# First projection of a two-layer transformer block: the bias of values and drift layer added by VectorE from a table on all partitions

## What is computed

```
Q = (x @ Wq + bq).reshape(B, S, Hn, Dh)
K = (x @ Wk + bk).reshape(B, S, Hn, Dh)
V = (x @ Wv + bv).reshape(B, S, Hn, Dh)
...
h = x @ dp_w1 + dp_b1
mu = h.mean(-1, keepdims=True)
var = ((h - mu) ** 2).mean(-1, keepdims=True)
h = (h - mu) / jnp.sqrt(var + LN_EPS) * ln_g + ln_b
```

## Time and profile before

| | |
|---|---|
| median of three runs | 3087.31 us (3075.47 to 3087.85) |
| the profiled execution, its time | 3087.55 us |
| its span in the trace | 3085.7 us |
| stage `project` in the trace | from about 31 to 205 us |
| mean granted clock of TensorE | 0.916 of full speed |

### The profile page before, as it was taken

The page is one execution under the profiler, slowest core; times in us unless marked ns, Lnnn a source line. Parts: engine busy times, 40 slices in busy tenths (PEclk is TensorE's granted clock), DMA queues, the critical chain, the costliest instruction groups (busy, mean ns, idle before and its releaser), DMA issues. The chain is left out here.

```text
span 3085.7 us, 91077 instructions
## 1 busy us (share of the span) xinstructions
PE 2676.6 (87%) x35080; PEld 1642.8 (53%) x35080; DVE 2270.2 (74%) x4339; ACT 1582.0 (51%) x2164; POOL 374.7 (12%) x341
## 2 busy tenths in 40 slices
PE   6869999899989998999999777999977778229997
PEld 3322566666656665567556424555535555117765
DVE  3539899799979987998989705565657897775776
ACT  2320677677767776777767671111115666204442
POOL 1245000000000000000000200000002222202333
PEclk9985899999999999999999897999988888659998
DMA  4244011101111011110110001000001222313341
GB/s 139 72 98 81 3 27 27 27 5 26 26 27 26 6 26 26 27 27 5 26 26 7 6 11 55 14 27 16 11 2 45 65 72 78 112 40 108 103 112 54
DMA packets 130633, 130.27 MB, mean 42 GB/s; under 512 B 76418, under 2 KB 107780, under 8 KB 125060
## 3 DMA queue, kind: packets, MB, share of 16 engines
q1 hardware_dynamic: 124548, 120.93, 16.6%
q10 hardware_dynamic: 4224, 4.19, 0.4%
q0 software_dynamic: 1536, 0.40, 0.1%
HBM read 78.41 MB, written 46.66 MB: 41 GB/s over the span
## 5 line engine op out<-in xcount | busy, mean ns | idle before, releaser
L677 DVE TENSOR_REDUCE attn_pm<-attn_MS 128x1 f32<-128x512 f32 (+3 forms) x2304 | 1334.0, 638 | 189.1 <-PE attn_MS L721 162.1
L661 ACT ACTIVATE attn_PT<-attn_ES 128x1024 f32<-128x1024 f32 (+5 forms) x1152 | 1039.1, 951 | 372.9 <-PE attn_ES L756 370.3
L721 PE MATMUL attn_MS<-attn_KX,attn_QX 96*32 96x512 bf16 (+11 forms) x9216 | 1038.3, 375 | 11.1 <-DVE attn_pm L677 5.6
L756 PE MATMUL attn_ES<-attn_QX,attn_KX 99*32 99x512 bf16 (+8 forms) x9216 | 773.0, 362 | 51.2 <-issue 20.1
L771 PE MATMUL attn_OP<-attn_PT,attn_VH 128*17 128x512 f32 (+3 forms) x4608 | 648.5, 565 | 0.2 <-ACT attn_PT L661 0.2
L721 PEld LDWEIGHTS attn_MS<-attn_KX,attn_QX 96*32 96x32 bf16 x9216 | 411.6, 97 | 300.7 <-issue 128.3
L756 PEld LDWEIGHTS attn_ES<-attn_QX,attn_KX 99*32 99x32 bf16 x9216 | 376.6, 97 | 194.7 <-ACT attn_PT L661 55.4
L1131 PE MATMUL l0out_ring<-l0out_w,l0out_sT 128*128 128x512 f32 x512 | 224.9, 592 | 0.0
L771 PEld LDWEIGHTS attn_OP<-attn_PT,attn_VH 128*17 128x17 f32 x4608 | 189.8, 98 | 48.9 <-issue 3.1
L716 PE MATMUL attn_MS<-attn_maskb,identb 128*32 128x128 bf16 (+3 forms) x2048 | 168.6, 206 | 37.8 <-DMA attn_QX<-qk_parts 25.4
L609 POOL TENSOR_SCALAR attn_parts<-attn_nmT 32x128 bf16<-32x128 f32 x16 | 22.6, 1411 | 1387.9 <-DVE attn_nmT L686 1387.9
(11 more groups left out here) (278 smaller groups left out, 2952.9 us busy)
## 6 DMA issues: line engine op xcount, KB each, us to landing
attn_KX<-qk_parts SPq DMA_DIRECT2D x96, 128.0 KB, 6.9
attn_QX<-qk_parts SPq DMA_DIRECT2D x96, 128.0 KB, 7.6
vk_beta<-front_vk SPq DMA_DIRECT2D x8, 1024.0 KB, 3.9
kq_transposed<-front_qkG SPq DMA_DIRECT2D x8, 1024.0 KB, 4.5
delta_VK<-vk_beta SPq DMA_DIRECT2D x32, 256.0 KB, 2.8
delta_QK<-kq_transposed SPq DMA_DIRECT2D x32, 256.0 KB, 2.9
attn_out<-attn_OS SPq DMA_DIRECT2D x128, 34.0 KB
x_res<-in_L_attn_x_dram ACTq DMA_DIRECT2D x8, 512.0 KB, 8.2
```

What stands on the lines that cost most here:

```text
L661: nc.scalar.activation(PT[u % NPT][:, 512 - wa:512 + wb], ES[half][:, 512 - wa:512 + wb], ACT.Exp, scale=DH ** -0.5).then_inc(exp_done, 1)
L677: nc.vector.tensor_reduce(pm[r][:, i, c:c + 1], MS[slot][:, 0:w], AX.X, ALU.max).then_inc(max_taken, 1)
L721: last = nc.tensor.matmul(MS[slot][r, 0:seen], QX[b][0:ROWS, i * P + 32 * g:i * P + 32 * g + 32], KX[b][0:ROWS, 512 * c:512 * c + seen], s ...
L756: last = nc.tensor.matmul(ES[half][r, o + past:o + w], KX[b][0:MAXR, kt * P + 32 * g:kt * P + 32 * g + 32], QX[b][0:MAXR, a + past:a + w], ...
```

## The change

The bias row `bvh` is loaded as a table that has the same 384 numbers on all 128 partitions. PE no longer makes the product of ones and bias; a vh group is the two products with the weights. VectorE replaces the copy of the values by an addition of the table (L325 in the new numbering) and, in place of the statistics from PSUM, adds the table to the drift columns and writes them to a new SBUF tile `hraw` (L328). The four statistics (L333) come after all four tiles and read `hraw`, as do the scaled rows `HD` (L344). There is one step more on VectorE, "hv", after which PSUM has been read for the last time in the turn; PE waits for "hv" and no longer for "hn" before it overwrites `vhp`. VectorE also waits for the weights' loads before its first instruction of the stage.

```diff
-    return wqk, wvh, flat[:, end:end + 4], flat[0:1, end + 4:end + 4 + E + HID]
+    return wqk, wvh, flat[:, end:end + 4], flat[:, end + 4:end + 4 + E + HID]
...
-            sp.dma_start(bvh[:, 0:E], d["L0_attn_bv"].rearrange("(o n) -> o n", o=1)).then_inc(wl, 16)
-            sp.dma_start(bvh[:, E:], d["L0_attn_dp_b1"].rearrange("(o n) -> o n", o=1)).then_inc(wl, 16)
+            sp.dma_start(bvh[:, 0:E], bcast(d["L0_attn_bv"], P)).then_inc(wl, 16)
+            sp.dma_start(bvh[:, E:], bcast(d["L0_attn_dp_b1"], P)).then_inc(wl, 16)
...
-    V = Steps("r1_0", "r1_1", "r1_2", "r1_3", "v", "haggr", "hrstd", "hn")
+    V = Steps("r1_0", "r1_1", "r1_2", "r1_3", "hv", "v", "haggr", "hrstd", "hn")
...
+        hraw = sb("hraw", [P, J, HID])
...
                 for j in range(J):
                     dve.wait_ge(md, M(g, f"vh_{j}"))
-                    nc.vector.tensor_copy(v17[:, bass.ds(g * J + j, 1), :, 0:DH],
-                                          vhp[:, j, 0:E].rearrange("p (o h c) -> p o h c", o=1, c=DH))
-                    last = nc.vector.bn_stats(hs6[:, j, :], vhp[:, j, E:E + HID])
+                    dve.sem_inc(held, 1)
+                    nc.vector.tensor_tensor(v17[:, bass.ds(g * J + j, 1), :, 0:DH],
+                                            vhp[:, j, 0:E].rearrange("p (o h c) -> p o h c", o=1, c=DH),
+                                            bvh[:, 0:E].rearrange("p (o h c) -> p o h c", o=1, c=DH), ALU.add)
+                    last = nc.vector.tensor_tensor(hraw[:, j, :], vhp[:, j, E:E + HID], bvh[:, E:], ALU.add)
+                last.then_inc(vd, 1)
+                dve.wait_ge(vd, V(g, "hv"))
+                dve.sem_inc(held, 1)
+                for j in range(J):
+                    last = nc.vector.bn_stats(hs6[:, j, :], hraw[:, j, :])
                 last.then_inc(vd, 1)
...
                     last = nc.vector.tensor_scalar(HD[:, bass.ds(g * J + j, 1), :],
-                                                   vhp[:, j, E:E + HID].rearrange("p (o c) -> p o c", o=1),
+                                                   hraw[:, j, :].rearrange("p (o c) -> p o c", o=1),
                                                    hmv[:, j, 0:1], hrs[:, j:j + 1], ALU.subtract, ALU.mult)
...
             dve.wait_ge(xl, 16 * G)
+            dve.wait_ge(wl, 16 * 8)
...
-                pe.wait_ge(vd, V(g - 1, "hn"))
+                pe.wait_ge(vd, V(g - 1, "hv"))
                 for j in range(J):
                     dst = vhp[:, j, 0:E + HID]
-                    nc.tensor.matmul(dst, k["ones"][0:1, :], bvh[:], start=True, stop=False)
                     for h in range(EH):
                         last = nc.tensor.matmul(dst, hT[:, h, j * P:(j + 1) * P], wvh[:, h, :],
-                                                start=False, stop=(h == 1))
+                                                start=(h == 0), stop=(h == 1))
                     last.then_inc(md, 1)
```

## The result

| | median of the runs | runs | profiled execution: span, granted clock |
|---|---|---|---|
| before | 3085.86 us | 4, 3075.47 to 3087.85 | 3085.7 us, 0.916 |
| after | 3119.95 us | 4, 3112.81 to 3126.14 | 3124.3 us, 0.902 |

The ratio is 1.0119, 95% interval 1.0092 to 1.0147: the change makes the kernel slower by 1.2%. The forecast was 3079.1 us, 3066 to 3088. The span grew by 38.6 us in the profiled executions, the medians by 34.1; the profiled execution after is the slowest of its four.

What follows compares the result with a forecast made beforehand. The stage was taken as bound by PE up to the last vh group, then by a VectorE and ScalarE chain. 18.1 us gained less 9.7 for the clock gave 8.4, so 3087.55 became 3079.1 us, range 3066 to 3088.

Steps and rivals of the forecast that it cites:

- these 174 us: Stage `project`, about 31 to 205 us, 6% of the span: any effect of the change must come out of it.
- The slower case: Whole kernel: slower by more than 0.5% (15.4 us) needs the lasting low clock or something unseen; chance 0.05.
- the price of a low start: Start of a turn at 1.2 GHz: 1.61 us lost each, six new ones, 9.7 us in all.
- TensorE saves 3.4 to 4.2 us per turn: Stage's vh groups: four bias groups fewer per turn save PE 3.4 to 4.2 us, not all of it gain.
- Additions at the price of what they replace: VectorE in the stage: two additions cost what copy and statistics did, so a tile keeps its 0.53 us.
- Tile 3 to the aggregation: VectorE at the turn's end: 1.80 us from tile 3's start to the aggregation, 1.03 more than before.
- A turn 2.18 us shorter at full clock: Stage's loop: aggregation starts 2.18 us earlier per turn, 15.3 us over seven turns.
- The last turn, 2.8 us: Stage's last turn, without `normalise`: PE's whole saving less 1.03 arrives, 2.4 to 3.2 us, taken as 2.8.
- TensorE idle for 3.3 to 4.1 us: End of each stage turn: PE's idle time grows from 2.14 to 3.3 to 4.1 us.
- All seven turns start at the low clock: Stage's loop: longer waits make all seven turns start at low clock, one already paid; loss 9.7 us.
- the second rival: Stage: clock returns more slowly, both first qk groups at 1.2 GHz, 2.8 us per turn; total 3087; chance 0.14.
- The table and the wait for it at nothing: Stage's start: 197 KB more loads and VectorE's wait for weights are hidden; without cover 0.6 us, once.

Runs made afterwards that it cites:

- the removal alone: Kernel before with TensorE's bias product left out, nothing in its place, bias not added: 3088.19 us, ratio 1.0002.
- the code put back: Changed kernel with 32 semaphore increments ahead of TensorE's attention code and 236 ahead of VectorE's: 3085.33 us, ratio 0.9993.
- the kernel with hint and order: Changed kernel, both codes put back by increments, with ScalarE's swapped order and the prefetch hint on TensorE's attention loop: 3037.22 us, ratio 0.9837.
- product kept: Changed kernel with the bias product on TensorE kept, so the bias is added twice: 3118.11 us, ratio 1.0103.
- shorter chain: Changed kernel, both codes put back, drift addition first, statistics tile by tile, tile 3's values addition behind the aggregation: 3076.29 us, ratio 0.9969.

## Why the prediction was wrong

**The step that failed** stands in the prediction's first paragraph: "Whatever it does must come out of these 174 us; the barrier behind the stage hands it on undiminished." The stage did hand on its gain, but the change also moved code, and no rival had that. By the runs, moving TensorE's code cost 28.0 us (3119.95 - 3091.96) and moving VectorE's 6.6 (3091.96 - 3085.33). Less the stage's 3 us of gain that is 31.6 of the 34.1 measured; the increments' own delay of 2.4 us would make up the rest, but that is also about what two groups of runs can differ by. The slower case had 0.05 of the chance, "the lasting low clock or something unseen". The clock didn't stay low through the stage's loop; it was the unseen.

A second step was mis-sized, the price of a low start, and it took most of the stage's gain; the list has it.

**Step by step in the stage:**
- TensorE saves 3.4 to 4.2 us per turn: right at the upper end. Without any wait at stake the turn fell by 4.14 us (19.62 to 15.48).
- Additions at the price of what they replace, a tile's pace of 0.53: right (157.84 - 157.31).
- Tile 3 to the aggregation, 1.80 us: 1.77. The statistics from SBUF took 0.87 for four, forecast 0.89. `HD` from SBUF takes 1.12 us for four, not 1.37.
- A turn 2.18 us shorter at full clock, so 18.0: right, by 17.0 of the removal alone and 1.00 for the chain. No turn of the change runs so, since its clock never held.
- The last turn, 2.8 us: 0.3 came (from the start of its qk groups to the aggregation 199.52 - 182.18 = 17.34, before 202.63 - 184.97 = 17.66), as its low clock took the rest.
- TensorE idle for 3.3 to 4.1 us: 4.15, at the top.
- All seven turns start at the low clock: right. **The price of 1.61 us was too small.** It was `hi_0` alone (here 165.69 - 161.79 = 3.90, forecast 3.7). But `hi_1` stands 6.69 us behind the start, against 4.25, 2.44 more: the low clock lasts into the second group. That was the second rival, 2.8 us per turn, with 0.14. (Its own terms, 6.9 us for eight halves and 0.4 behind them, give 7.3 us and not the 7.05 that it states; 6.69 was measured.) By the durations of their qk halves (10.28 against 7.83 in the turn shown) the seven turns lost 16.8 us, of which the kernel before had paid 1.6 once (9.45 in the earlier trace rows). 18.1 - 15.2 leaves 2.9 us, and the stage shows about 3.
- The table and the wait for it at nothing: first statistics at 32.40 instead of 32.14, so 0.26 us at most.

With the code put back, 3085.3 us were measured. That is inside the range around 3079.1, but by the slow clock's mechanism and not by the forecast's, so it would have been luck.

That all seven turns would start low was the author's estimate, from one low start in seven behind waits of 2.2 us. In the changed kernel all seven do, behind 4.07 to 4.16 us. A wait of more than 2.2 us alone doesn't do it: the removal alone waits 3.06 to 3.15 us in every turn, and its clock holds from the third on (PEclk 1.00 from 65 to 180.8 us).

## What to carry to other kernels

An edit in one stage moves the code of all that follows on the same engine. Here that cost 28.0 us in a long, straight loop, where the stage gained 3. So compare the two traces outside the stage too, look for waits put down to "issue" that come back at the same place of each turn, and test them by putting the removed number of instructions back at a place where the engine waits anyway. Two repairs helped here: gaps in the load bursts, in which instruction packets came (2 in the 12 us where there had been none; 45 us faster than the changed kernel), and the hint at the long loop's branch (14 us). And before work is moved onto an engine whose result closes the turn, look for the queue order that puts it there: here moving one call on ScalarE, with the codes put back, turned a change that gave 3 us in its stage into one worth 28.

## What the runs showed of the hardware

- TensorE waited for its instructions, at branches and in straight code. At each branch back it paused for 5.9 to 6.7 us before, and for at most 0.3 with the hint (one of 3.2 us in the kernel with hint and order). In straight code it paused for 2.3 to 5.1 us in mid-turn in the kernel after (up to 6.2 in the removal alone), the first time with the DMA engines 99% busy with loads, and not when the loads were spread. In the kernel after, an instruction packet of 1.7 to 1.9 us ended 1.4 to 1.5 us before the end of each mid-turn pause. Why a place of 11 lets one packet through in the burst and a place of 235 none isn't shown.
- The low clock and the idle time ahead of a turn didn't go together one to one: 3.15 us of idle time with the clock held from the third turn on (removal alone), 3.34 us with it low in every turn (product kept), and 3.71 us with longer and shorter low stretches in turn (shorter chain).
- VectorE too has pauses that nothing in the profile released: 2.5 to 2.9 us at each of its four branches back in attention, and by the place of its code four more of 2.0 to 2.3 us just behind them. They stay when the loads are spread (13 pauses, 19.9 us).
